# Convolution phase on four 64x64 TensorE tiles with two images at a time, in place of 128x128 matmuls with an fp32r high and low part

## The reference, cut to what matters

```python
def _ln_c(v, eps=1e-06):                       # over the 64 channels of each pixel
    m = jnp.mean(v, axis=1, keepdims=True)
    ...
# x: (32, 64, 56, 56) float32; weight: (64, 64, 3, 3)
bwq = binary_quantize(bw) * sw                 # sign of the centred weight, times a power of two
ba = binary_quantize(x)                        # sign of the normalised input
y = jax.lax.conv_general_dilated(ba, bwq, window_strides=(1, 1), padding=((1, 1), (1, 1)), ...)
yn = (y - mean) * jax.lax.rsqrt(var + BN_EPS)  # batch norm over all images and pixels
yn = yn * gamma.reshape(1, -1, 1, 1) + beta.reshape(1, -1, 1, 1)
return jnp.clip(yn, -1.0, 1.0)
...
x = x + _L0_conv_ref(_ln_c(x), ...)
t = _to_tokens(x)
t = t + _L0_ffn_ref(_ln_t(t), ...)             # 8 experts: 64->64, relu, 64->64, relu, 64->64, gated
x = _from_tokens(t, x)
```

## Time and profile before

| what | value |
|---|---|
| median of 3 runs | 1423.2 us (1422.77 to 1428.34) |
| the profiled execution's own time | 1421.64 us |
| its span, first to last instruction | 1419.7 us |
| mean granted TensorE clock | 0.984 |
| TensorE matmul busy | 1344.9 us, 95% |
| VectorE, ScalarE, GpSimd busy | 971.1, 885.3, 553.2 us |
| convolution phase | about 0 to 213 us of the span |
| expert phase with its prologue | 213 us to the end |

### The profile page before, as it was taken

How to read it: one execution, slowest core, us unless ns; L and a number is a source line. 1 busy time by engine, 2 the same in 40 slices (tenths; PEclk the granted TensorE clock), 3 DMA queues, 4 the chain that set the end, 5 groups by cost and what they waited for, 6 DMA issues and landing times. The chain is left out here.

```text
span 1419.7 us, 34136 instructions
## 1 busy us (share of the span) xinstructions
PE 1344.9 (95%) x12984; PEld 667.3 (47%) x12984; DVE 971.1 (68%) x1660; ACT 885.3 (62%) x1279; POOL 553.2 (39%) x474
## 2 busy tenths in 40 slices
PE   3999973999999999999999999999999999999998
PEld 2666651544444544445444444444544454444444
DVE  5888872676767666666666666676766767666665
ACT  3666664666666666656666666666666666666653
POOL 7000052434444443444343344444434444434441
PEclk9999995999999999999999999999999999999999
DMA  9999931232233333223333233233333323332221
GB/s 159 176 151 149 143 52 27 60 79 61 55 71 67 73 73 80 52 61 73 67 72 75 61 65 68 62 78 69 77 66 61 66 60 73 73 80 48 53 49 32
DMA packets 361597, 107.08 MB, mean 75 GB/s; under 512 B 353552, under 2 KB 353776, under 8 KB 361456
## 3 DMA queue, kind: packets, MB, share of 16 engines
q1 hardware_dynamic: 360192, 103.49, 38.9%
q0 software_dynamic: 1264, 1.61, 0.7%
HBM read 78.97 MB, written 26.09 MB: 74 GB/s over the span
## 5 line engine op out<-in xcount | busy, mean ns | idle before, releaser
L936 DVE SCALAR_TENSOR_TENSOR v<-ps,negb,wb 128x448 f32<-128x448 f32 x896 | 571.0, 678 | 300.9 <-PE ps L572 300.1
L743 ACT ACTIVATE h<-ps,bias 128x896 f32<-128x896 f32 x448 | 451.3, 1007 | 318.9 <-PE ps L550 318.9
L550 PE MATMUL ps<-xc,w 64*64 64x448 f32 x3584 | 458.1, 541 | 13.1 <-POOL xc L435 11.3
L588 PE MATMUL ps<-v,wo 64*64 64x448 f32 x3584 | 454.7, 540 | 3.4 <-issue 2.9
L572 PE MATMUL ps<-h,w 64*64 64x448 f32 x3584 | 450.9, 540 | 4.9 <-issue 2.5
L588 PEld LDWEIGHTS ps<-v,wo 64*64 64x64 f32 x3584 | 169.9, 133 | 187.5 <-issue 174.6
L550 PEld LDWEIGHTS ps<-xc,w 64*64 64x64 f32 x3584 | 162.3, 132 | 185.2 <-issue 179.4
L572 PEld LDWEIGHTS ps<-h,w 64*64 64x64 f32 x3584 | 166.0, 133 | 160.3 <-issue 146.7
L465 POOL TENSOR_TENSOR o<-o,upper 128x448 f32<-128x448 f32 x112 | 127.4, 1137 | 284.3 <-DVE o L946 284.3
L457 POOL TENSOR_TENSOR o<-xin,gconst 128x448 f32<-128x448 f32 x112 | 130.2, 1182 | 236.0 <-ACT gconst L786 143.3
L435 POOL TENSOR_TENSOR xc<-xc,spread 128x896 f32<-128x896 f32 x56 | 121.5, 2187 | 172.0 <-DMA spread<-rs_rows 172.0
(11 more groups left out here) (151 smaller groups left out, 837.8 us busy)
## 6 DMA issues: line engine op xcount, KB each, us to landing
xa<-in_x SPq DMA_DIRECT2D x64, 392.0 KB, 6.3
xin<-in_x SPq DMA_DIRECT2D x112, 224.0 KB, 4.1
spread<-rs_rows SPq DMA_DIRECT2D x112, 224.0 KB, 4.1
out<-o SPq DMA_DIRECT2D x224, 112.0 KB, 2.5
rs_rows<-rs SPq DMA_DIRECT2D x112, 3.5 KB
rows<-in_L_ffn_g POOLq DMA_DIRECT2D x2, 256.0 KB, 6.1
rows<-in_L_ffn_v POOLq DMA_DIRECT2D x2, 256.0 KB, 7.2
cwt<-in_L_conv_weight SPq DMA_DIRECT2D x2, 144.0 KB, 2.6
```

What stands on the lines that cost most here:

```text
L550: last = mm(ps[64 * two:64 * two + 64, L1_BANKS + ab, 0:NG], w1[half, P * q + C * two:P * q + C * two + C], xc[half, s, g // 2, ab ^ (g % ...
L588: last = mm(ps[64 * par:64 * par + 64, ACC_BANKS + low, 0:NG], wo[rows_, 2 * Q + d, :], v[rows_, u % 2, par ^ (g % 2), d, :], start=(Q == ...
L743: A(h[:, u % 2, i], ps[:, L1_BANKS:L1_BANKS + 2, 0:NG], ACT.Relu, bias=bias[:, 0, q:q + 1]).then_inc(h_done[i], 1)
L936: last = V.scalar_tensor_tensor(out=v[:, u % 2, ab, d, :].rearrange("p (b w) -> p b w", w=W), in0=ps[:, L2_BANKS[ab] + d, 0:NG].rearrange( ...
```

## The change

The convolution phase is written anew; the expert phase stays, except that its chunk k now holds rows k and 28 + k of all images in place of rows 2k and 2k + 1 (L287 and L312 read and write other rows, with pieces of 224 B as before).

- A step now takes two images (`TWOS` = 16 pairs). Four DMAs load a pair: 64 partitions each, and one contiguous piece of 28 x 56 float32 = 6272 B for each partition. Upper and lower half of an image lie on the two partition halves. `xa` has three buffers of a pair in place of four of one image.
- Centring is done in fp32 on the loaded data, with `centre64` on four 64x64 tiles, in groups of 7 rows (392 columns): four matmuls a group, four groups a pair. `xhi`, `xlo`, the fp32r matrix and VectorE's split are gone.
- The output tile of a centring matmul is chosen so that one image ends up on each partition half; ScalarE writes the signs of a group with one instruction over two PSUM banks (784 elements) to `sgn`, which now holds whole images of 58 x 58.
- The convolution is nine taps of 64x64 bf16 weights on four tiles: 36 matmuls of 392 columns for a group of 7 rows in both halves of two images. ScalarE keeps a group with one instruction over two banks, VectorE does two bn_stats for it.
- TensorE's order is now by group: centre group g of pair m + 1, then convolve group g of pair m. PSUM has two buffers of two banks for each of both. ScalarE follows in the same order; its `fold_roots` comes behind pair 8.
- All 16 pairs are unrolled; there is no hardware loop.
- GpSimd's weight DMAs wait until the first pair has been loaded. The loads of `xin` wait until 15 of 16 pairs are centred.

```diff
-SLOTS = RP + 1
-TAPS = 9
+KERNEL = 3
+TAPS = KERNEL * KERNEL
 GA = 4
 KG = RP // GA
-XRING = 4
+NA = KG * W
+TWOS = B // 2
+XRING = 3
+SRING = 2
+TILES = ((0, 0), (1, 1), (0, 1), (1, 0))
...
-                def load_image(b, slot):
-
-                    xb = x_pairs[b] if isinstance(b, int) else x_pairs[bass.ds(b, 1)].rearrange("o c k t w -> (o c) k t w")
-                    sp.dma_start(xa[0:64, slot, 1:SLOTS, :], xb[:, :, 1, :]).then_inc(s_xa[slot], 16)
-                    sp.dma_start(xa[64:128, slot, 0:RP, :], xb[:, :, 0, :]).then_inc(s_xa[slot], 16)
-
-                sp.wait_ge(s_zero, 1)
-                for b in range(XRING):
-                    load_image(b, b)
-                with sp.Fori(0, B // XRING - 1) as r:
-                    for i in range(XRING):
-                        sp.wait_ge(a_split, XRING * r + i + 1)
-                        load_image(XRING * r + XRING + i, i)
+                def load_images(m):
+
+                    if m >= XRING:
+                        sp.wait_ge(a_centred, GA * (m - XRING) + GA)
+                    for n in range(2):
+                        for h in range(2):
+                            xb = x[2 * m + (n ^ h), :, RP * h:RP * h + RP, :].rearrange("c k w -> c (k w)")
+                            sp.dma_start(xa[64 * h:64 * h + 64, xa_slot(m), n].rearrange("p g e -> p (g e)"), xb).then_inc(s_xa[xa_slot(m)], 16)
+
+                for m in range(TWOS):
+                    load_images(m)
...
-                sp.wait_ge(a_split, B - XRING + XIN_OVER)
+                        sp.dma_start(xin[64 * h:64 * h + 64, s, images], x[images, :, RP * h + q, :].rearrange("b c w -> c b w")).then_inc(x_loaded[p], 16)
+
+                sp.wait_ge(a_centred, GA * (TWOS - 1))
...
+                pool.wait_ge(s_xa[xa_slot(0)], N_XA)
                 for i, vec in enumerate((g1, v1, g2, v2)):
                     dma(rows[:, i, :], vec.rearrange("(o e) h -> o (e h)", o=1).broadcast_to([P, E * C])).then_inc(s_ffn, 16)
...
-                def centre_image(b, i):
-                    pe.wait_ge(a_split, b + 1)
+
+                def centre_images(m, g):
+
+                    if g == 0:
+                        pe.wait_ge(s_xa[xa_slot(m)], N_XA * (m // XRING) + N_XA)
+                    pe.wait_ge(a_signed, GA * m + g + 1)
+                    pe.sem_inc(a_free, 1)
+                    for low, high in TILES:
+                        rows_ = slice(64 * low, 64 * low + 64)
+                        last = mm(ps[64 * high:64 * high + 64, A_BANKS[g % 2] + low, 0:NA], centre64[rows_, :],
+                                  xa[rows_, xa_slot(m), low ^ high, g, :], start=True, stop=True)
+                    last.then_inc(a_centred, 1)
+
+                def conv_images(m, g):
+
+                    if g == 0:
+                        pe.wait_ge(a_signed, GA * m + GA + 2)
+                    pe.wait_ge(a_kept, GA * m + g + 1)
+                    pe.sem_inc(a_free, 1)
+                    for tap in range(TAPS):
+                        ky, kx = tap // KERNEL, tap % KERNEL
+                        for low, high in TILES:
+                            rows_ = slice(64 * low, 64 * low + 64)
+                            top = RP * high + KG * g + ky
+                            last = mm(ps[64 * high:64 * high + 64, CONV_BANKS[g % 2] + low, 0:NA], convw[rows_, tap, :],
+                                      sgn[rows_, m % SRING, top:top + KG, kx:kx + W], start=(tap == 0), stop=(tap == TAPS - 1))
+                    last.then_inc(a_conv, 1)
+
+                pe.wait_ge(s_centre, 1)
+                for g in range(GA):
+                    centre_images(0, g)
+                pe.wait_ge(s_act, 3)
+                for m in range(TWOS):
                     for g in range(GA):
-                        lo, hi = slot_group(g)
-                        pe.wait_ge(a_signed, GA * b + g + 1)
-                        at = ps[:, g, 0:(hi - lo) * W]
-                        mm(at, centre[:], xhi[:, i % 2, lo:hi, :], start=True, stop=False)
-                        mm(at, centre[:], xlo[:, i % 2, lo:hi, :], start=False, stop=True).then_inc(a_centred, 1)
-
-                def conv_image(b, i):
-                    for g in range(GA):
-                        pe.wait_ge(a_signed, GA * b + g + 1 + RINGA)
-                        pe.wait_ge(a_kept, GA * b + g + 1)
-                        at = ps[:, GA + g, 0:KG * W]
-                        for kx in range(3):
-                            for nxt in range(2):
-                                last = mm(at, convw[:, kx, nxt, :], sgn[:, i % 2, KG * g + nxt:KG * g + nxt + KG, kx:kx + W],
-                                          start=(kx + nxt == 0), stop=(kx + nxt == 3))
-                        last.then_inc(a_conv, 1)
-
-                pe.wait_ge(s_act, 3)
-                centre_image(0, 0)
-
-                def image(b, i, r, left):
-                    if not isinstance(b, int) or left:
-                        centre_image(b + 1, i + 1)
-                    conv_image(b, i)
-
-                body_of_images(pe, image)
+                        if m + 1 < TWOS:
+                            centre_images(m + 1, g)
+                        conv_images(m, g)
...
-                def sign_image(b, i):
-                    act.wait_ge(a_conv, GA * b + GA)
-                    for g in range(GA):
-                        lo, hi = slot_group(g)
...
-                    for g in range(GA):
-                        act.wait_ge(a_conv, GA * b + g + 1 + RINGS)
-                        yb = y[:, KG * g:KG * g + KG, b, :] if isinstance(b, int) else \
-                            y[:, KG * g:KG * g + KG, bass.ds(b, 1), :].rearrange("p k o w -> p (k o) w")
-                        A(yb, ps[:, GA + g, 0:KG * W].rearrange("p (k w) -> p k w", w=W), ACT.Copy).then_inc(a_kept, 1)
...
+                def sign_images(m, g):
+                    if g == 0 and m >= SRING:
+                        act.wait_ge(a_conv, GA * (m - SRING) + GA)
+                    act.wait_ge(a_centred, GA * m + g + 1)
+                    rows_ = sgn[:, m % SRING, 1:H + 1, 1:W + 1].rearrange("p (two k) w -> p two k w", two=2)
+                    A(rows_[:, :, KG * g:KG * g + KG, :], ps[:, A_BANKS[g % 2]:A_BANKS[g % 2] + 2, 0:NA].rearrange("p a (k w) -> p a k w", w=W),
+                      ACT.Sign).then_inc(a_signed, 1)
+
+                def keep_images(m, g):
+                    act.wait_ge(a_conv, GA * m + g + 1)
+                    A(y[:, KG * g:KG * g + KG, 2 * m:2 * m + 2, :].rearrange("p k b w -> p b k w"),
+                      ps[:, CONV_BANKS[g % 2]:CONV_BANKS[g % 2] + 2, 0:NA].rearrange("p b (k w) -> p b k w", w=W), ACT.Copy).then_inc(a_kept, 1)
...
+                act.wait_ge(s_zero, 2)
+                for g in range(GA):
+                    sign_images(0, g)
+                for m in range(TWOS):
+                    for g in range(GA):
+                        if m + 1 < TWOS:
+                            sign_images(m + 1, g)
+                        keep_images(m, g)
+                    if m == TWOS // 2:
+                        fold_roots()
                 act.preload_act_table_set("sqrt_and_others")
-                act.wait_ge(a_stats, B + 5)
+                act.wait_ge(a_stats, TWOS + 5)
...
-                V.tensor_tensor(centre[:], ident[:], ones64[:], ALU.subtract)
-
-                def split(b, i, r):
-                    s4 = i % XRING
-                    dve.wait_ge(s_xa[s4], 32 * (r + i // XRING) + 32)
-                    if not (isinstance(b, int) and b < 2):
-                        dve.wait_ge(a_centred, GA * b - GA)
-                    V.tensor_copy(xhi[:, i % 2], xa[:, s4]).then_inc(a_hi, 1)
-                    dve.wait_ge(a_hi, b + 1)
-                    V.tensor_tensor(xlo[:, i % 2], xa[:, s4], xhi[:, i % 2].bitcast(F32), ALU.subtract).then_inc(a_split, 1)
-
...
+                    last = V.tensor_tensor(centre64[half, :], ident[half, half], ones64[half, half], ALU.subtract)
+                last.then_inc(s_centre, 1)
+
+                def image_stats(m, g):
+                    dve.wait_ge(a_kept, GA * m + g + 3)
+                    for b in range(2 * m, 2 * m + 2):
+                        last = V.bn_stats(stats[:, b, g, :], y[:, KG * g:KG * g + KG, b, :])
+                    if g == GA - 1:
+                        last.then_inc(a_stats, 1)
...
+                for m in range(TWOS):
+                    for g in range(GA):
+                        image_stats(m, g)
```

More of the change, by code:

```diff
@@ L70, in metaformer_kernel @@
         halves = sb("halves", [P, P], F32)
-        convw = sb("convw", [P, 3, 2, P], BF16)
+        convw = sb("convw", [P, TAPS, C], BF16)
         w1 = sb("w1", [P, E * C], F32)
@@ L105, in metaformer_kernel @@
         cwa = sb("cwa", [P, C * TAPS], F32, early)
-        cwsign = sb("cwsign", [C, 3, 5, C], BF16, early)
+        cwsign = sb("cwsign", [C, KERNEL, KERNEL, C], BF16, early)
         identb = sb("identb", [C, C], BF16, early)
```

(15 more changed lines are left out.)

82 lines of the change are left out of this document (21 added, 61 removed).

## The result

The kernel after took 1415.62 us (median of 8 runs, 1407.76 to 1416.75), the kernel before 1425.85 us in the same session (8 runs, 1422.77 to 1429.38). The ratio is 0.9915, 95% interval 0.989 to 0.9939: faster by 0.85%, some 10 us, where 42 to 45 had been forecast. The profiled execution took 1413.79 us with a span of 1411.7.

What follows compares the result with a forecast made beforehand. TensorE was taken to bound the convolution phase; its end 42.1 us earlier, less 0.9 for the tail, gave net 41.2 us: 1421.6 - 41.2 = 1380.4, rounded to 1381 us (own range 1370 to 1390; 8 in 10: 1368 to 1412).

Steps and rivals of the forecast that it cites:

- The price of a set: Convolution on TensorE: four bf16 tiles of 392 columns run side by side in 0.168 us (bounds 0.164 to 0.336).
- (b): Rival, convolution: sets stretched to 0.20 us by weight load and waits between groups; 1398 us; chance 0.13.
- (e): Rival, convolution: tiles run two at a time at full column rate, 0.336 us a set; 1478 us, slower; chance 0.08.
- issue (31 ns an instruction): Rival, convolution: instruction issue binds in a steady stream, 0.248 us a set; 1427 us, no change; chance 0.05.
- the weight load: Rival, convolution: load not hidden under the set before, 0.318 us a set; 1467 us, slower; chance 0.06.
- Rival (a): Image loads bound the convolution phase at 173 GB/s: end 15 us later than forecast, 1396 us; chance 0.10.
- pair 1: Start of the convolution phase: this pair's loads, sharing the engines with weight loads, arrive at 23 us (20 to 25).
- the tail: End of the convolution phase: from last convolution matmul to bn_aggr 2.05 us instead of 1.17, 0.9 more.
- the first centring: Start of the convolution phase: the first pair's loads arrive, so its centring can begin, at about 13 us.
- `fold_roots` costs TensorE: Convolution phase: ScalarE's 2.8 us piece stalls TensorE 1 us, once (0 to 2.8).
- The sum: Convolution phase: 25 + 15 x 8.67 + 4 x 1.51 + 1 = 162.1 us for the last convolution matmul, against 204.2.
- the expert phase "at nothing": Expert phase: only the rows loaded and stored change, hidden by idle DMA share; cost nothing, 1214.3 us from bn_aggr to end.

Runs made afterwards that it cites:

- e1: Kernel after the change without the image loads of pairs 3 to 15 and TensorE's waits for them, computing on old data: 1387.78 us, ratio 0.9742 to before.
- e3: Kernel before the change with only the expert phase's rows (loads and stores) changed as in the kernel after: 1424.48 us, ratio 0.9996 to before.
- e9: Kernel after the change with 48 more TensorE instructions without effect between convolution and expert phase: 1404.75 us, ratio 0.9859 to before.
- e10: Kernel after the change with 24 more TensorE instructions without effect between convolution and expert phase: 1407.81 us, ratio 0.9865 to before.
- e5_pe_loop4: Kernel after the change with TensorE's pairs in a hardware loop of four pairs a round and four buffers of `xa`: 1394.21 us, ratio 0.9769 to before.
- e7_pad: Kernel after the change with 896 B a partition of unused memory put in front: 1407.27 us, ratio 0.9869 to before.
- e6: Kernel after the change with TensorE's pairs in a hardware loop of two, two `xa` buffers, `xin` loads awaiting the last pair: 1386.5 us, ratio 0.9721 to before.

## Why the prediction was wrong, by its own steps

**Right.** The price of a set, on which all was said to hang: 0.168 us forecast, and the step of 2.17 us is measured to the hundredth. Rivals (b) to (e) are out: e1 runs sets back to back for 100 us, so neither issue (31 ns an instruction) nor the weight load nor two tiles at a time binds. Rival (a) is out as worded: behind pair 1 TensorE waits for loads once, 1.2 us. In a steady stream 36 matmuls take 1.51 us, 42 ns each. The 62 ns a matmul that the Trainium skill gives for hardware decoding off ("TensorE: Matmul & The Clock Gate", Part 1) don't bind here; no run shows which way of decoding was on. ScalarE (0.82), VectorE (1.04 for 1.12), the tail (1.96 for 2.05) and the first centring (13.6 for 13) are right. Two small terms came out lower: pair 1 was there at 20.8, not 23, and `fold_roots` costs TensorE about 0.1 us and not 1 (window 100 to 120 us of e1: 19.92 busy). Without the stalls the stream ends at 160.6 (e1), where 162.1 was forecast.

**Wrong, first step: "The sum", 15 x 8.67.** It took for granted that a step without a wait takes as long as its matmuls. I priced the issue of an instruction (12 to 47 ns) and asked whether the sequencer could send them, but not where they come from. The change does to the supply of instructions two things at once, more than three times the rate (12 to 41 a us) and no loop, and it keeps the engines that bring them full with larger bursts. I even noted that the loads fit in 7.1 of 8.67 us, and took "hidden" to mean that they disturb nobody. Missing term: ten late blocks, about 20 us of stalls and some 3 us of lower clock behind them (granted 0.91 in the windows 40 to 60 and 140 to 160 us). The last convolution matmul starts at 184.2 against 160.2 in e1, 24.0 us. Since the sum was 1.5 us too long otherwise, the end was missed by 22.4 us (184.5 for 162.1).

**Wrong, second step: the expert phase "at nothing".** I priced only the other rows, and rightly at nothing (e3). The instructions there are the same, but their place within the blocks is not. The phase is 10.7 us longer between the two profiled executions (1193.8 against 1183.1), and 8.0 us of it is seen as gaps inside layers, all but one with an instruction packet in front. The medians say somewhat less: the profiled executions lie 4.2 us under the median before and 1.8 us under the median after, so about 8 us is the fair figure. That late blocks lengthen this phase is shown; that the shifted borders alone explain the difference is supported by e9 and e10, on one profile each.

Together 22.4 + 10.7 = 33.1 us, where the profiled execution is 33.4 us over its forecast (1413.8 and 1380.4).

The Trainium skill ("Runtime: NRT & Kernel Launch", Instruction fetch mechanics) says that blocks are of 16 KB, that the crossing of a border is mostly hidden, and that kernels prefer full unrolling. The size agrees with the packets of q8 (15 packets, 0.25 MB, in e1). The second agrees with e1, where fifteen blocks cost nothing. It does not hold where the DMA engines are full and TensorE consumes 41 instructions a us (up to 4.4 us for a block, in e5_pe_loop4), and as to the third the loop of two pairs is 28 us faster than the unrolled form (ratios 0.9721 and 0.9915). The page gives TensorE room for 2048 instructions; that 1470 stay for the next round in e5 agrees.

**Left open.** How far ahead a block is asked for: the profile shows when its transfer starts, not the request. Why blocks are late in the expert phase with idle DMA engines. Why e7_pad gained 7 to 8 us. And the kernel after has two groups of runs, 1408 and 1415 us, of which the profile caught one.

## What to carry to other kernels

When an edit makes instructions shorter or more numerous, count instructions per us and ask whether they are unrolled and what else is on the DMA engines: gaps marked "issue" between two matmuls with no semaphore between them, which end 2 to 3 us after the start of a packet of the instruction queue, were late blocks here. The cures seen are a hardware loop short enough to be kept (28 us), or giving transfers out one at a time instead of in bursts (16 to 18 us). A change of a few us in an untouched, unrolled phase may be nothing but a shift of its code; before explaining it, shift it on purpose, and compare medians, since one profile of such a phase can be several us off.

## What the runs showed of the hardware that was not expected

- Four 64x64 tiles in bf16 with 392 columns run side by side at 0.168 us a set (42 ns a matmul) with their weight loads hidden, for as long as instructions are there.
- A late block left TensorE standing for 0.7 to 4.4 us in the convolution phase; after a stall of 3.3 us (start to start, at 37.9) the lower clock level followed (granted 0.57 from 41 to 45 us), after one of 3.5 us at 56.9 it did not (1.00 from 60 to 80 us).
- Late blocks are there in the kernel before as well: nine in its expert phase, at a mean DMA share of 0.31.
- 48 instructions without any effect, put in an idle stretch, made the kernel 8 to 11 us faster (ratios to before 0.9859 and 0.9915; medians 1404.75 and 1415.62 from two sessions).
- Images in pieces of 6272 B, beside the weight loads, moved at 206 to 212 GB/s at a share of 1.03 to 1.04, and alone at 183 GB/s at 0.81 (e6); pieces of 224 B at 147 at a share of 1.00.
